# A graph transformer layer: the prefill of the expert slots in the loop over head pairs, edge ranges on TensorE and VectorE, and two narrow one-hots as one comparison

## What is computed

```python
xn = layernorm(x)
# 1. graph convolution with self loops, normalised by the degrees of the source nodes
h = xn @ W.T + b;  deg = zeros.at[row].add(1);  norm = deg[row]**-0.5 * deg[col]**-0.5
gnn = segment_sum(norm[:, None] * h[col], row)          # row = src, col = dst, and (i, i)
# 2. linear attention, 16 heads of 64, 256 random features
phi(y) = (exp(y @ orf.T / 64**0.25 - |y|**2 / (2 * 64**0.5)) + 1e-6) / sqrt(256)
mix = (phi(q) @ (phi(k).T @ v)) / (phi(q) @ sum(phi(k))) @ Wo.T + bo
x = x + gnn + mix
# 3. mixture of 8 experts, the best 2 of each node, softmax over the two
x = x + sum_e gate_e * (layernorm(x) @ expert_w[e] + expert_b[e])
```

## Time and profile before

| | |
|---|---|
| Median of 3 runs | 1686.0 us (1684.91 to 1687.53) |
| The profiled execution | 1684.43 us |
| Its span in the profile | 1682.3 us, 25130 instructions |
| Mean granted TensorE clock | 0.954 |
| PE busy | 1477.8 us (88%) |
| DVE busy | 747.2 us (44%) |
| ACT busy | 436.9 us (26%) |
| POOL busy | 343.4 us (20%) |
| Chain that ended last | PE 82%, DVE 5%, issue 4%, unknown queue 2%, DMA 2% |
| DMA queue q1 | 48096 packets, 127.20 MB |

### The profile page before, as it was taken

The page is one execution under the profiler, slowest core; times in us unless marked ns, Lnnn a source line. Parts: engine busy times, 40 slices in busy tenths (PEclk is TensorE's granted clock), DMA queues, the critical chain, the costliest instruction groups (busy, mean ns, idle before and its releaser), DMA issues.

```text
span 1682.3 us, 25130 instructions
## 1 busy us (share of the span) xinstructions
PE 1477.8 (88%) x7987; PEld 1219.1 (72%) x8051; DVE 747.2 (44%) x1413; ACT 436.9 (26%) x727; POOL 343.4 (20%) x333
## 2 busy tenths in 40 slices
PE   4718788899998999999999999998999589999990
PEld 1406667664446999999999999997788578888870
DVE  6805555412002454544544444444545514554436
ACT  6300111111001333332333232333213202332320
POOL 5510212112310111010110101000413311212233
PEclk9959999999999999999999999999999679999995
DMA  3580001141211000000000000000432515566648
GB/s 144 190 287 10 22 5 35 35 144 63 94 63 35 26 23 19 21 25 12 25 12 25 25 12 25 0 1 19 127 125 95 200 56 206 194 237 246 234 167 298
DMA packets 54830, 150.64 MB, mean 90 GB/s; under 512 B 7130, under 2 KB 14250, under 8 KB 54480
## 3 DMA queue, kind: packets, MB, share of 16 engines
q1 hardware_dynamic: 48096, 127.20, 21.5%
q0 software_dynamic: 6688, 22.83, 4.3%
HBM read 119.72 MB, written 48.64 MB: 100 GB/s over the span
## 4 chain that ended last, share of the span: by engine, by line
PE 82%; DVE 5%; issue 4%; another core or an unknown queue 2%; DMA 2%; ACT 2%; POOL 2%; DVEq 1%; POOLq 0%; SPq 0%; ACTq 0%
PE PB L1406 10%; PE PB L1435 7%; PE PB L1437 7%; PE PB L1436 7%; PE PB L1611 5%; PE PB L1612 5%; PE PB L1614 5%; PE PB L1471 4%; PE PB L1494 4%; PE PB L1356 4%; PE PB L1394 2%; PE PB L1417 2%; PE PB L1395 2%; PE PB L1396 2%
## 5 line engine op out<-in xcount | busy, mean ns | idle before, releaser
L1435 PE MATMUL PB<-xh,hw 128*128 128x416 f32 (+1 forms) x576 | 206.0, 358 | 4.9 <-POOL orfl L692 4.9
L1437 PE MATMUL PB<-xh,hw 128*128 128x416 f32 (+1 forms) x576 | 204.1, 354 | 0.0
L1436 PE MATMUL PB<-xl,hw 128*128 128x416 f32 (+1 forms) x576 | 203.9, 354 | 0.0
L1406 PE MATMUL PB<-h,AT 128*128 128x512 f32 x400 | 171.9, 592 | 1.2 <-ACT h L835 1.2
L1611 PE MATMUL PB<-mwh,mth 128*128 128x512 f32 x368 | 149.0, 405 | 1.3 <-issue 1.3
L1406 PEld LDWEIGHTS PB<-h,AT 128*128 128x128 f32 x400 | 75.9, 190 | 96.5 <-issue 94.6
L1612 PE MATMUL PB<-mwl,mth 128*128 128x512 f32 x368 | 144.6, 393 | 0.0
L1356 PE MATMUL PB<-ohs,ohd 128*128 x471 | 103.6, 342 | 42.4 <-DVE ohs L1031 29.1
L1394 PE MATMUL PB<-wqh,xh 128*128 128x256 f32 x320 | 93.5, 292 | 41.6 <-ACT h L829 39.9
L1029 DVE TENSOR_SCALAR ohd<-iota,dc 128x128 f16 x178 | 69.1, 388 | 134.0 <-PE PB L1356 122.3
L658 POOL CAST hw<-hraw 128x1024 fp32r<-128x1024 f32 x24 | 24.9, 1038 | 477.8 <-PE PB L1437 469.5
(11 more groups left out here) (230 smaller groups left out, 2837.6 us busy)
## 6 DMA issues: line engine op xcount, KB each, us to landing
mraw<-expert_w SPq DMA_DIRECT2D x64, 512.0 KB, 5.4
slot_y<-ybuf SPq DMA_DIRECT2D x46, 256.0 KB, 3.4
xrow<-x SPq DMA_DIRECT2D x20, 256.0 KB, 2.7
y_scratch<-xrow SPq DMA_DIRECT2D x20, 256.0 KB, 2.0
yrow<-y_scratch SPq DMA_DIRECT2D x20, 256.0 KB, 2.8
x2n_half<-xhat SPq DMA_DIRECT2D x20, 256.0 KB, 2.5
out<-x SPq DMA_DIRECT2D x9, 512.0 KB
AT<-wg SPq DMA_DIRECT2D x32, 128.0 KB, 2.2
```

The lines of the kernel that those rows point to most:

```text
L1406: ins = mm(bank(4 + u % 2), AT[:, b, t * P:(t + 1) * P], hh[c][:, b, :], start=(b == 0), stop=(b == TT - 1))
L1435: mm(bank(i, n), hw[:, wi, 0, k, :], xh[:, k, c0:c0 + n], start=(k == 0), stop=False)
L1436: mm(bank(i, n), hw[:, wi, 0, k, :], xl[:, k, c0:c0 + n], start=False, stop=False)
L1437: ins = mm(bank(i, n), hw[:, wi, 1, k, :], xh[:, k, c0:c0 + n], start=False, stop=(k == KT - 1))
```

## The change

Three edits:

- The four fills of `slot_y` ahead of the second quarter are gone. In the loop over head pairs 1 to 7, after the load of the third head weight, SyncE issues one fill of 640 rows (`FILL` = 4480 / 7). The wait ahead of the experts counts seven DMAs instead of four.
- `partition_all_reduce` is gone. TensorE transposes `ext` into PSUM bank 6, VectorE takes the maximum along the free axis (`extm`, 20 partitions), TensorE turns this column into one row in bank 7 by a matmul with the identity, and VectorE reads it there. TensorE does this ahead of its wait for `s_rng`.
- `dc`, the dst column values, is float16 instead of float32. Both `ohd` of a chunk pair are made by one comparison of two tensors (the 128 node numbers repeated twice against two dst columns, each repeated 128 times), after one wait for both slots. The two `ohs` stay as they are, behind it.

```diff
+FILL = MAXT * P // (KT - 1)
@@ SyncE
-                if i == KT:
-                    for r0 in range(0, MAXT * P, NP):
-                        n = min(NP, MAXT * P - r0)
-                        sp.dma_start(slot_y[r0:r0 + n, :], x[0:n, :]).then_inc(slots_filled, 16)
@@ SyncE, in the loop over j = 1 to 7, after the three loads of hraw
+                sp.dma_start(slot_y[ds((j - 1) * FILL, FILL), :], x[0:FILL, :]).then_inc(slots_filled, 16)
@@
-            sp.wait_ge(slots_filled, 16 * -(-MAXT * P // NP))
+            sp.wait_ge(slots_filled, 16 * (KT - 1))
@@ GpSimd
-            pool.wait_ge(s_ext, 1)
-            g.partition_all_reduce(extr[:, :], ext[:, :], PAIRS, RMAX).then_inc(s_extr, 1)
@@ VectorE
             dve.wait_ge(s_extr, 1)
+            v.tensor_reduce(extm[:, :], PB[0:2 * TT, 512 * 6:512 * 6 + PAIRS], AX.X, ALU.max).then_inc(s_extm, 1)
+            dve.wait_ge(s_extr, 2)
+            extr = bank(7, 2 * TT)
@@ VectorE, one_hots
+                    dve.wait_ge(oh_free, 2 * (begin + i) + 2)
+                    v.tensor_tensor(ohd[:, ds(2 * side, 2), :],
+                                    iota[:, b * P:(b + 1) * P].rearrange("p (a n) -> p a n", a=1).broadcast_to([P, 2, P]),
+                                    dc[:, ds(2 * at, 2)].rearrange("p (a n) -> p a n", n=1).broadcast_to([P, 2, P]), ALU.is_equal)
                     for p in range(2):
                         col = 2 * at + p
-                        dve.wait_ge(oh_free, 2 * (begin + i) + p + 1)
-                        v.tensor_scalar(ohd[:, ds(2 * side + p, 1), :].rearrange("p a n -> p (a n)"),
-                                        iota[:, b * P:(b + 1) * P], dc[:, ds(col, 1)], None, ALU.is_equal)
@@ TensorE
+            pe.wait_ge(s_cst2, 9)
+            pe.wait_ge(s_ext, 1)
+            nc.tensor.transpose(PB[0:2 * TT, 512 * 6:512 * 6 + PAIRS], ext[:, :], ident[0:PAIRS, 0:PAIRS]).then_inc(s_extr, 1)
+            pe.wait_ge(s_extm, 1)
+            mm(PB[0:1, 512 * 7:512 * 7 + 2 * TT], extm[:, :], ident[0:2 * TT, 0:2 * TT], start=True, stop=True).then_inc(s_extr, 1)
             pe.wait_ge(s_rng, 1)
-            pe.wait_ge(s_cst2, 9)
```

More of the change, by code:

```diff
@@ L24 @@
 MAXT = (2 * N + 2 * (P - 1)) // P + 1 + 2 * (E - 2) + 1
+FILL = MAXT * P // (KT - 1)
+assert FILL * (KT - 1) == MAXT * P and FILL <= NP
 CHUNKS = ((0, 512), (512, 512), (1024, NP - 1024))
@@ L50 @@
 ds = bass.ds
-RMAX = bass.bass_isa.ReduceOp.max
 def gps_layer(nc, x, dst_pairs, src_cols, dst_cols, wg, bg, wq, bq, wk, bk, wv, bv, wo, bo, orf,
@@ L89, in gps_layer @@
         sc = keep("sc", [P, 2 * PAIRS], F32, s1)
-        dc = keep("dc", [P, 2 * PAIRS], F32, s1)
+        dc = keep("dc", [P, 2 * PAIRS], F16, s1)
         s1.close()
@@ L140, in gps_layer @@
         ext = keep("ext", [PAIRS, 2 * TT], F32, pb)
-        extr = keep("extr", [PAIRS, 2 * TT], F32, pb)
+        extm = keep("extm", [2 * TT, 1], F32, pb)
         rng = keep("rng", [1, 4, TT], F32, pb)
@@ L254, in gps_layer @@
         s_extr = sem("s_extr")
+        s_extm = sem("s_extm")
         s_rng = sem("s_rng")
```

## The result

The changed kernel takes 1641.1 us (median of 4 runs, 1638.8 to 1643.5); the kernel before took 1686.8 beside it (4 runs, 1684.9 to 1690.2). The ratio is 0.9727, 95% interval 0.9705 to 0.9749. 1640.0 had been predicted, with a range of 1635 to 1650.

A forecast was written before the change was run, and what follows sets the result against it. Bound by TensorE and the one-hots up to 450 us, with a 38.5 us weight wait behind fills and a GpSimd wait at the start. 37.75 + 1.25 + 7.1 - 0.2 = 45.9 saved, giving 1640.0 us, range 1635 to 1650.

The forecast's parts named there:

- 37.75 for the stall: Before TensorE's third tile: without the fills ahead, the second quarter's weights land early, saving 37.75 us of waiting.
- 1.25 for the clock: TensorE's third tile: full clock instead of half saves 2.25 us, 1.0 given back in the block behind, net 1.25.
- The stall put at 0.2: Before TensorE's third tile: 0.2 us of waiting left, as one-hots of the next block can lengthen GpSimd's part; bounds 0 and 3.
- the cover of 0.6: At the third tile: ScalarE's chain ends at 87.49, TensorE's second tile at 88.09, so just covered, by 0.6 us.
- the 6.29 of the sum: Second quarter: 6.29 us from ScalarE's first copy to TensorE's third tile, half of the weights still to be fetched.
- Rival 3: Second quarter's weights were late because the ring waited for GpSimd; only the start is won, 1679 us; chance 0.02.
- The fills in the loop: Loop over head pairs: seven fills of 8.0 us each lie beside other work, cost 0; cover gone over some 55 us.
- Edge ranges: At the start: replacing GpSimd's reduction takes 1.85 us, first rng operation at 9.3 instead of 16.43, saving 7.1; bounds 5.3 and 8.9.
- None of them becomes late: Block 0: GpSimd's normalisation starts 14 us earlier, first quarter's weights follow it, and none of these is late.
- One-hots: Range-sum pairs: one comparison of 0.42 us replaces two operations; +0.5 from fewer GpSimd waits in block 0, -0.2 us in all.
- Rival 4: Every pair of all blocks: comparison far dearer, TensorE waits beyond 0.69 us; slower than before, 1694 at 1.3; chance 0.03 with anything else slower.
- Rival 2: More gained, 1632 to 1636 us: block 0 loses its 1.6 of waits and pairs come closer than 1.71; chance 0.12.

The follow-up runs named there:

- the first kernel: The kernel before with only the fills of slot_y moved into the loop over head pairs: 1646.3 us, ratio 0.9758.
- late: Changed kernel with GpSimd's conversions of the first quarter's weights, and half of ScalarE's, put behind block 0: 1637.7 us, ratio 0.9721.
- both further edits: Changed kernel with those GpSimd and half of ScalarE's conversions behind block 0, and normalisation of x on ScalarE: 1636.5 us, ratio 0.971.

## Why the prediction was right, step by step

**Fills.** 37.75 for the stall and 1.25 for the clock, 39.0 together. The part alone measured 40.0; in the trace the way from first tile to block 1 fell from 49.0 to 8.7, 40.3, of which 1.0 was given back in block 1, as predicted: 39.3 (block 1 with its tiles was 29.3 us long before and is 30.2 now: 86.37 to 116.6). No stall is left before the third tile: ScalarE started the second quarter at 76.50 and had ended it at 82.58. The stall put at 0.2 did not come, and the cover of 0.6 held: TensorE ended its second tile at about 83.5. ScalarE did wait for weights in between, 3.2 us in four pieces, as the ring of four slots had made it do before (2.8), and that was inside the 6.29 of the sum. Rival 3 has fallen with the first kernel: the stall went with nothing but the fills moved. A half of it was true, though, and I had not seen it. Where the fills stood in time was GpSimd's doing, so before the change each microsecond that GpSimd won or lost in block 0 was one of the total.

**The fills in the loop.** Cost 0, right: head loads land after 3.3 us as before. 8.0 us per fill was right back to back (8.2 measured), 11.7 from issue to landing. "The cover would be gone with a fill of over 55 us": it was just not gone with seven fills of 8.2, 58 us.

**Edge ranges.** Predicted 9.3 for the first rng operation, measured 8.24. The replacement takes 0.9 us from 7.37 on, where I had 1.85: hand-overs from 7.66 to 7.70 and from 7.93 to 7.98 are half as long as the 0.1 I had put for each, the transpose is 0.29 and not 0.5, the one-row matmul 0.22 and not 0.7 (the weight loads add nearly nothing), and `ext` was ready a little earlier. The first pair of block 0 came 7.2 earlier, against 7.1 predicted; but by two errors that cancel, and that is luck. 8.2 were won at rng, and 0.9 of them lost again at the first two wide one-hots, which took 1.87 together beside GpSimd's normalisation. That meeting is chance: in the kernel with six more fills, the same up to there, and in "late" they took 1.01 and the first pair stood at 13.7. The start before scatters as well: with the fills alone, where nothing is changed up to there, the first pair stood at 20.7 and not at 21.9. GpSimd had been moved 15 us ahead by the same edit, "None of them becomes late" was all that I asked of it, and not what it would meet there.

**One-hots.** Predicted -0.2 in all, with +0.5 in block 0 for meeting GpSimd less often. That step failed. The edit costs about 2.5 us in this trace: 0.9 at the first pair, 1.5 in block 0 (49.0 against 47.5 without it); in the trace with six more fills the two are 0.1 and 0.8, and the medians put the edit at 1.2, within their scatter. I had counted the operations that meet GpSimd, three in place of four, and taken from the count that less time is lost. It was not: beside the conversions of weights every form was longer than in the quiet. The comparison took 0.94 us instead of 0.42, and the two wide one-hots behind it 1.94 instead of 1.01. In the kernel with fills and ranges alone the narrow one-hots took 0.71 beside the same conversions instead of 0.25, and single wide ones up to 1.09 instead of 0.55; here is its VectorE timeline, and the windows view of TensorE there:

```profile
40.55 1.08 DVE L1031 TENSOR_SCALAR ohs<-iota,sc 128x1280 f16 x1
41.55 0.71 DVE L1029 TENSOR_SCALAR ohd<-iota,dc 128x128 f16 x1
42.18 1.06 DVE L1031 TENSOR_SCALAR ohs<-iota,sc 128x1280 f16 x1
43.16 0.71 DVE L1029 TENSOR_SCALAR ohd<-iota,dc 128x128 f16 x1
...
40.00:48.00 8.00, 4.14 (x19) 1.79 (x19) 8.00 (x12) 1.67 (x4) 7.08 (x9) 1.00 0.35 105
```

Measured against pairs 1.70 apart, TensorE fell behind by 3.1 us beside the conversions in the changed kernel, and by 2.7 both in this one and in the one with six more fills. So the conversions cost nearly the same with either form. Of the 1.5 us, 0.6 were lost ahead of them, beside the normalisation, 0.4 beside them, and 0.5 behind them, where TensorE's clock was down. Of the seven traces in which the comparison ran beside GpSimd's conversions, six have a stretch of 3 us or more at 1.2 GHz in block 0 (the one without is that with six more fills), and of the seven with the narrow one-hots of before or with the conversions put late none has. What brings the clock down stays open, though: the last line above has TensorE busy for 4.14 of 8 us, as little as the 4.08 of the changed kernel, and its clock stayed at 1.00 then and after. The Trainium skill (SBUF — State Buffer, section "SBUF: two separate sides") has the lock on the shared ports also for an operation with two SBUF inputs, and by it the new comparison would still wait for GpSimd; the trace agrees, with 0.94 against 0.42. I had cited that rule and counted on a gain all the same. Outside block 0 the step was right: the comparison is 0.42 long, pairs are 1.69 apart, and 0.34 of VectorE is idle.

**Rivals.** Rival 4 was well placed: at a comparison of 0.69 the pace outside block 0 is still the old one, and with 0.60 us more work per pair it is not. Its price per pair was too high: it gives 2.13 for the two comparisons, and 1.85 was measured, since an operation's record is 0.08 longer than the time it holds VectorE and the 0.08 put for the loop are not seen. Rival 2 did not happen in this kernel, for the reason above. Its first half did in the one with both further edits, block 0 without waits, at 1636.5, half a microsecond above the 1632 to 1636 that it gave; pairs came no closer than 1.70 in any kernel.

**The sum.** In the trace: 7.2 at the first pair, -2.6 in block 0 and 40.3 behind it are 44.9 at block 1, and 44.5 at the product with `AT` (351.4 to 306.9). The profiled execution ended only 42.3 earlier, since one head pair (545.9 to 628.5) took 82.6 us where the others take 80:

```profile
590.00:605.00 15.00, 14.13 (x97) 13.03 (x96) 4.28 (x9) 3.60 (x6) 3.43 (x2) 0.94 0.43 141
605.00:620.00 15.00, 15.00 (x81) 14.88 (x81) 5.54 (x12) 5.26 (x9) 0.00 (x0) 0.84 0.16 68
```

The granted clock, 0.94 and 0.84 in these windows, is what cost the time, and not the fill: every pair has one, the other pairs last 80.0 as before, and the kernel with seven fills per pair has a granted clock of 1.00 in every window from 545 to 1000 us. The medians, 45.7 apart, are nearer to the forecast of 46 than this one execution. That they are so near is in part luck: term by term the traces have 7.2 for 7.1 and 39.3 for 39.0, but -2.6 in block 0 for -0.2, which ended at 63.6 and not near 60.8. The 2.6 are 1.5 of the one-hot edit and 1.1 that the block lost with the narrow one-hots too (47.5 against 46.3), once the ranges had moved GpSimd's work; the prediction had nothing for the latter. One of its signs of being wrong, a head pair of more than 80 us, did show, and came from the clock.

## What to carry to other kernels

A transfer that nobody waits for can cost its whole length if loads that someone does wait for stand behind it in the same queue; ask of each such transfer what is behind it, and when the one that frees its place will let it go, since its start can hang on an engine that looks idle. An operation that is cheap in the quiet can have a second price beside GpSimd, whichever form it has, and when an edit moves GpSimd's work in time, look at what it will meet. And effects measured one by one add up only when they don't share a stall: here 61 us of parts made 46.

## What the runs showed of the chip

- A comparison of two 16-bit tensors with broadcast inputs took 0.42 us for 256 elements per partition and 0.69 for 512, about 0.15 us + 1.0 ns per element. With the same fixed part the wide comparison against a column (0.55 for 1280) is at 0.3 ns per element. The Trainium skill's table (VectorE: DVE Perf Modes, section "The perf-mode tier table") has a factor of two between the forms; these rows have over three, and they decide here.
- Copies of 2.62 MB from DRAM to DRAM took 8.2 us each back to back, and one alone 11.7 from issue to landing. With the DMA engines full at 327 GB/s TensorE's granted clock stayed at 1.00 and its pace in the blocks as it was.
- VectorE beside GpSimd: a comparison against a column of 1280 elements, 0.55 us in the quiet, took 3.25 in block 3 beside GpSimd's adding of 1280 float32 elements per partition (L631, 2.9 to 3.3 us long), and the comparison of two tensors up to 3.0. Both forms wait.
- TensorE's granted clock falls to the 1.2 GHz level for 3 to 10 us in places that differ from trace to trace: block 0, a tile, block 3, one head pair. In block 0 of the changed kernel TensorE had been idle for half of the 8 us before it, but it was so in a kernel whose clock stayed up; in the head pair it had been busy for over 90% of the time. The cause stays open. Such a stretch cost 0.5 us (block 0 of the changed kernel) to 2.6 (the head pair), about the scatter of the runs.
- An engine took up another's result within 0.05 us in the chain of three that replaced the reduction over partitions; behind the reduction itself, whose record is 0.43, the next GpSimd operation began only 7.4 us later.
